# The last batch's attention across heads, set at other steps of the four queues

## What is computed

```python
def _L0_cond2_ref(x, s, ...):
    kx = modulated_linear(x, s, k_aff_w, k_aff_b, k_w, k_b)
    kx = kx.reshape(B, N, H, D)          # 16 heads of 16 features
    q = k = v = kx
    scores = jnp.einsum('bnhd,bnjd->bnhj', q, k) / math.sqrt(D)
    A = jax.nn.softmax(scores, axis=-1)
    out = jnp.einsum('bnhj,bnjd->bnhd', A, v).reshape(B, N, F)
    return modulated_linear(out, s, o_aff_w, o_aff_b, o_w, o_b)
...
for i in range(DEPTH):                   # DEPTH = 6
    x = attn_layer(shift_tokens(x), ...) + x
    x = ffn_layer(shift_tokens(x), ...) + x
```

## Time and profile before

| what | value |
| --- | --- |
| median of 3 runs | 3278.33 us |
| lowest and highest run | 3275.71 and 3279.32 us |
| span of the profiled execution | 3280.4 us |
| TensorE busy | 3087.2 us (94%) |
| VectorE busy | 2638.4 us (80%) |
| ScalarE busy | 2534.1 us (77%) |
| GpSimd busy | 2084.0 us (64%) |

### The profile page before, as it was taken

The page is one execution under the profiler, slowest core; times in us unless marked ns, Lnnn a source line. Parts: engine busy times, 40 slices in busy tenths (PEclk is TensorE's granted clock), DMA queues, the critical chain, the costliest instruction groups (busy, mean ns, idle before and its releaser), DMA issues. The chain is left out here.

```text
span 3280.4 us, 80720 instructions
## 1 busy us (share of the span) xinstructions
PE 3087.2 (94%) x29936; PEld 2736.1 (83%) x29936; DVE 2638.4 (80%) x5117; ACT 2534.1 (77%) x7059; POOL 2084.0 (64%) x1536
## 2 busy tenths in 40 slices
PE   5898886689999999999999999999999999999997
PEld 4666664479998999989999989999899998999996
DVE  3378888878789888788878898878988878888884
ACT  2787885478787888788888888888788887888784
POOL 5347655776666666666666676667676767666661
PEclk8888996799999999999999999999999999999998
DMA  3111100110001000001100011000100000110000
GB/s 128 55 36 49 59 4 7 42 36 11 2 2 34 25 26 2 2 21 33 31 2 2 11 34 39 1 2 2 37 26 22 2 1 21 33 31 7 8 5 26
DMA packets 27780, 75.04 MB, mean 23 GB/s; under 512 B 4120, under 2 KB 9848, under 8 KB 27256
## 3 DMA queue, kind: packets, MB, share of 16 engines
q1 hardware_dynamic: 22224, 52.63, 5.1%
q0 software_dynamic: 4864, 16.78, 1.6%
q10 hardware_dynamic: 304, 0.47, 0.1%
HBM read 65.68 MB, written 4.19 MB: 21 GB/s over the span
## 5 line engine op out<-in xcount | busy, mean ns | idle before, releaser
L1596 POOL TENSOR_TENSOR turned<-by_cos,turned 128x512 f32<-128x512 f32 x384 | 494.5, 1288 | 827.5 <-DVE turned L2101 827.0
L1600 POOL TENSOR_TENSOR rnorm<-norm,half 128x8 f32<-128x8 f32 x384 | 789.1, 2055 | 0.0
L1883 ACT ACTIVATE prob<-ps_s,ebias,rnorm 128x128 f32<-128x128 f32 x1536 | 681.8, 457 | 64.9 <-DVE ebias L2122 64.2
L2115 DVE TENSOR_REDUCE negmax<-ps_s 128x8 f32<-128x1024 f32 x192 | 235.0, 1224 | 284.0 <-PE ps_s L1698 283.9
L1892 ACT ACTIVATE prob_t<-ps_t 128x512 f32<-128x512 f32 x384 | 230.3, 600 | 223.4 <-PE ps_t L1707 218.8
L2130 DVE TENSOR_TENSOR prob<-prob,rinv 128x512 f32<-128x512 f32 x384 | 375.8, 979 | 13.1
L1642 PE MATMUL ps_qk<-w_hi,x_hi 128*128 128x512 f32 x768 | 336.8, 438 | 18.8 <-DVE turned L2101 12.2
L1787 PE MATMUL ps_f<-hid_hi,w_hi 128*128 128x256 f32 (+1 forms) x1056 | 309.3, 293 | 5.7 <-DVE hid_lo L2176 5.6
L1883 ACT ACTIVATION_READ_ACCUMULATOR prob<-ps_s,ebias,rnorm 128x1 f32 x1536 | 311.1, 203 | 0.0
L1642 PE MATMUL ps_qk<-w_lo,x_hi 128*128 128x512 f32 x768 | 305.8, 398 | 0.0
L1642 PE MATMUL ps_qk<-w_hi,x_lo 128*128 128x512 f32 x768 | 305.7, 398 | 0.0
(11 more groups left out here) (289 smaller groups left out, 9779.6 us busy)
## 6 DMA issues: line engine op xcount, KB each, us to landing
w_raw<-in_w_qkv SPq DMA_DIRECT2D x24, 768.0 KB, 4.8
w_raw<-in_w SPq DMA_DIRECT2D x12, 693.0 KB, 4.0
w_raw<-in_w_o SPq DMA_DIRECT2D x12, 512.0 KB, 3.4
w_raw<-in_w SPq DMA_DIRECT2D x6, 768.0 KB, 4.4
x_tok<-in_x SPq DMA_DIRECT2D x8, 256.0 KB, 2.7
kept<-x_t SPq DMA_DIRECT2D x8, 256.0 KB, 2.0
w_raw<-kept SPq DMA_DIRECT2D x8, 256.0 KB, 3.1
out<-rows_out SPq DMA_DIRECT2D x8, 256.0 KB, 2.2
```

The source lines that it names most:

```text
L1596: G.tensor_tensor(turned[:, k, :], by_cos[:, :], turned[:, k, :], ALU.add).then_inc(s["turned"], 1)
L1600: G.tensor_tensor(rnorm[:, i % RR, :], norm2[:, k, :], half[:, :], ALU.pow).then_inc(s["rnorm"], 1)
L1883: last = A.activation(prob[:, k, h, :], half_bank(h % 2, k)[:, T(h // 2)], ACT.Exp, bias=ebias[:, i // NU % 2, k, h:h + 1], scale=rnorm[:, ...
L2115: V.tensor_reduce(negmax[:, k, :, :].rearrange("p u (c o) -> p o u c", o=2), ps_s[:, :, :].rearrange("p o (u c k) -> p o u c k", u=NU, c=2 ...
```

## The change

Nothing is added and nothing taken away. Lines of the form `for c in lates(...)` get other offsets and other places in the lists of POOL, TensorE, ScalarE and VectorE. The offsets, before and after (VectorE unless another engine is named):

| piece | unit 0: before, after | unit 1: before, after |
| --- | --- | --- |
| `head_prod` 0, 1, 2, 3 | 0 0 0 1, 0 0 0 1 | 2 2 3 4, 3 3 4 5 |
| `head_scores` 0, 1, 2, 3 | 0 0 1 1, 0 0 1 1 | 3 4 4 4, 3 4 5 5 |
| `head_mirror` (ScalarE) | 2, 0 | 5, 6 |
| `head_peak` | 2, 1 | 7, 6 |
| `head_exp` (ScalarE) | 2, 1 | 8, 6 |
| `head_weights` | 2, 3 | 8, 8 |
| `head_out` 0, 1, 2, 3 (POOL) | 4 6 6 8, 4 5 6 7 | 10 10 13 15, 10 11 13 15 |
| `head_out` 0, 1, 2, 3 | 3 4 7 8, 4 5 7 9 | 9 9 13 13, 9 12 14 14 |

The other offsets stay (`turn_k` 1, `flip_heads` 13 and `heads_out` 14 of TensorE, `flip_heads` 13 and `heads_out` 15 of ScalarE), but the places in a step change. An offset alone doesn't place a piece: one at the head of a step's list stands just behind one at the foot of the step before. The core of the diff, of which the rest is like it:

```diff
@@ pe @@
         for t in range(STEPS):
+            for c in lates(t, 14):
+                heads_out(c)
             for q in passes(t, 20):
...
-            for c in lates(t, 14):
-                heads_out(c)
             for i in units(t, 0):
                 project(i)
@@ dve @@
-            for c in lates(t, 9):
-                head_out(c, 1, 1)
+            for c in lates(t, 12):
+                head_out(c, 1, 1)
```

More of the change, by code:

```diff
@@ L1606, in pool @@
         for t in range(STEPS):
[L1607 to L1608 removed]
+            for c in lates(t, 1):
+                turn_k(c)
+            for c in lates(t, 10):
+                head_out(c, 1, 0)
+            for c in lates(t, 15):
+                head_out(c, 1, 3)
+            for c in lates(t, 5):
+                head_out(c, 0, 1)
+            for i in units(t, 3):
+                rotated(i)
+            for c in lates(t, 7):
+                head_out(c, 0, 3)
+            for c in lates(t, 11):
+                head_out(c, 1, 1)
+            for q in passes(t, 25):
+                hidden_lo(q, 0)
+            for c in lates(t, 4):
+                head_out(c, 0, 0)
+            for q in passes(t, 20):
+                inverse_root(q)
+            for c in lates(t, 13):
+                head_out(c, 1, 2)
             for c in lates(t, 6):
                 head_out(c, 0, 2)
[L1611 to L1630 removed]
             for q in passes(t, 27):
@@ L1833, in pe @@
                 mean_mm(q)
+            for c in lates(t, 13):
+                flip_heads(c)
             for q in passes(t, 14):
@@ L1837, in pe @@
                 w_o_mm(q, 1)
-            for c in lates(t, 13):
-                flip_heads(c)
             for q in passes(t, 21):
@@ L1967, in act @@
                 soften(i)
-            for c in lates(t, 2):
-                head_mirror(c, 0)
             for q in passes(t, 20):
@@ L1979, in act @@
                 attend(r)
-            for c in lates(t, 2):
-                head_exp(c, 0)
             for q in passes(t, 21):
@@ L1999, in act @@
                 flip_prob(i)
+            for c in lates(t, 0):
+                head_mirror(c, 0)
             for layer in layers(t, 16):
                 w1_high(layer, 0)
+            for c in lates(t, 13):
+                flip_heads(c)
             for layer in layers(t, 18):
@@ L2005, in act @@
                 w_o_high(layer, 1)
-            for c in lates(t, 15):
-                heads_out(c)
             for q in passes(t, 17):
                 square(q)
-            for c in lates(t, 13):
-                flip_heads(c)
+            for c in lates(t, 6):
+                head_exp(c, 1)
             for layer in layers(t, 20):
@@ L2015, in act @@
                 gelu(q, 1)
+            for c in lates(t, 1):
+                head_exp(c, 0)
     def dve():
@@ L2317, in dve @@
                 attend_lo(r)
-            for c in lates(t, 3):
-                head_prod(c, 1, 2)
+            for c in lates(t, 0):
+                head_prod(c, 0, 2)
             for q in passes(t, 22):
@@ L2323, in dve @@
                 linear_lo(q)
-            for c in lates(t, 7):
-                head_out(c, 0, 2)
             for c in lates(t, 1):
-                head_scores(c, 0, 3)
+                head_peak(c, 0)
     sp()
```

124 lines of the change are left out of this document (52 added, 72 removed).

## The result

| what | before | after |
| --- | --- | --- |
| median of 8 runs | 3277.02 us | 3282.86 us |
| lowest and highest run | 3270.48 and 3280.89 us | 3273.36 and 3287.09 us |
| ratio, 95% interval | | 1.0025, 1.0013 to 1.0037 |
| repeated, medians of 17 and 12 runs | 3274.97 us | 3278.58 us |
| ratio of the repeat, 95% interval | | 1.0015, 1.0000 to 1.0029 |

The forecast was 3278.1 us, range 3273.9 to 3281.5, and "no difference" at 0.93. The time is outside the range, on the slow side, and the interval of the first comparison lies above 1. The change is a small loss: by the two ratios 0.15 to 0.25%, so 5 to 8 us (the medians themselves lie 5.84 and 3.61 us apart). The miss of the range by 1.4 us is itself no measure, since the repeat, at 3278.58 us, lies inside it while the kernel before came out at 3274.97; what has to be explained is the difference.

What follows compares the result with a forecast made beforehand. VectorE bounds 590 to 645 us, a two-step loop paces 645 to 710, TensorE is 98.5% busy after. Terms -0.7 + 0.5 + 0 = -0.2 us give 3278.1 us against the runs' median 3278.33; range 3273.9 to 3281.5.

Steps and rivals of the forecast that it cites:

- Part 1: Steps 8 to 10: `soften(3)` and `rotate(9)` start earlier, TensorE's wait for POOL's keys goes; 0.7 us gained, bounds 0 to 0.94.
- Part 2: Step 14: `heads_out` first in TensorE's queue, so the transposes of `flip_qk(12)` come later; +0.5 us, bounds 0 to 0.8.
- Part 3: Steps 0 to 7: VectorE's reordered late work costs about nothing; 0, bounds 3.0 us lost to 1.1 us gained.
- The collision with `turn_k`: Start of the layers: the first `head_prod` stands 1.0 us for POOL's `turn_k`, the state's cast 0.8 less; sum 0.2 us higher.
- the term 0: Steps 0 to 7: the moved VectorE work was taken to cost 0 us in sum.
- fewer collisions: Steps 0 to 7: pieces might run into fewer collisions, gaining one late sum, 1.1 us; the gain bound.
- the 2.12 us of `weigh(2)`: `weigh(2)` on VectorE, slow beside POOL's late product; product leaves, but `soften(2)` waits for scores anyway, so given nothing.
- the bound of 3.0: Steps 0 to 7: 2.09 + 0.87 = 3.0 us lost if all of it opens as idle time.
- the rival that named the clock: Steps 8, 10, 12: less TensorE waiting keeps the clock up, three projections give 4.2 us, 3273.9 us; chance 0.14.
- Slower from the start: Steps 0 and 1: first square later than `rotate(0)` can be, second `project` delayed; 3.0 us lost, 3281.1 us; chance 0.2.
- The moves cancel: Step 10's wait comes back one step later, leaving only Part 2's loss; 3278.8 us; chance 0.2.

Runs made afterwards that it cites:

- a_again: The changed kernel profiled again with no edit; 3278.58 us (median of 12 runs), `rotate(20)` +5.34 us against before.
- a_pe: The changed kernel with TensorE's queue as before (transposes of `flip_qk(12)` ahead of `heads_out`); 3278.88 us, `rotate(20)` +7.40 us.
- b_fill: The kernel before with POOL's late products of the last batch replaced by constant fills that only write; 3275.46 us, `rotate(20)` +1.20 us.
- a_pool: The changed kernel with POOL's products of unit 0 back where the kernel before has them; 3270.11 us, `rotate(20)` +0.42 us.
- a_fill: The changed kernel with POOL's late products of the last batch replaced by constant fills that only write; 3278.57 us, `rotate(20)` +3.84 us.
- best: a_pool with `head_weights` of unit 1 moved behind `soften(2)`; 3275.80 us (median of 12 runs), ratio to before 1.0009.
- a_o2: The changed kernel with only POOL's third product of unit 0 moved ahead of `rotated(3)`; 3294.68 us, `rotate(20)` +5.62 us.
- late: The kernel before with only the later half of the change, steps 0 to 5 and TensorE's queue as before; 3280.47 us, `rotate(20)` +0.37 us.
- b_again: The kernel before profiled again with no edit; 3268.89 us, `rotate(20)` +0.34 us against its first profile.
- the pair of fills: The kernels before and after, each with POOL's late products of the last batch replaced by constant fills; 3275.46 and 3278.57 us.

## Why the prediction was wrong

**What bounds the kernel.** Read right: from 710 us on nothing changed, and between 590 and 645 us VectorE bounds. That reading should have warned: where VectorE bounds, each of its instructions that takes longer is on the path.

**Part 1, forecast -0.7 us: right in its steps, too large in size.** From `rotate(7)` to `rotate(9)` it takes 13.84 us now, against 14.36: 0.52 us gained in this profile and 0.21 in a_again. VectorE, `rotate(7)`, the split with the wait for ScalarE's copy that was foreseen, and `rotate(9)`:

```profile
648.85 0.69 DVE L2095 TENSOR_TENSOR by_cos<-ps_qk,cos_t 128x512 f32<-128x512 f32 x1
...
658.74 1.22 DVE L2054 TENSOR_TENSOR wo_lo<-w_raw,wo_hi 128x1024 fp32r<-128x1024 f32 x1 [0.44 <-ACT wo_hi L1920]
...
662.69 0.68 DVE L2095 TENSOR_TENSOR by_cos<-ps_qk,cos_t 128x512 f32<-128x512 f32 x1
```

The idle time ahead of `soften(4)` is 1.22 us, forecast about 1.3, where it was 2.46:

```profile
674.49 1.22 DVE L2115 TENSOR_REDUCE negmax<-ps_s 128x8 f32<-128x1024 f32 x1 [1.22 <-PE ps_s L1698]
```

TensorE's wait of 2.42 us for POOL's keys ahead of `flip_qk(8)` is gone too: it follows at 655.66 us with 1.14 us of idle for ScalarE. Each step of this part held. What it left out is a wait that took the place of the work that went from ahead of `rotate(8)`:

```profile
653.92 0.69 DVE L2095 TENSOR_TENSOR by_cos<-ps_qk,cos_t 128x512 f32<-128x512 f32 x1 [1.20 <-ACT sq L1856]
```

**Part 2, forecast +0.5 us: right.** `heads_out` waits 1.16 us now (0.19 before) with the transposes behind it, `rotate(14)` is 0.43 us later against `rotate(13)`, and a_pe, without the move, has -0.01.

```profile
688.78 1.99 PE L672 MATMUL bank_m<-o_t,o_w 128*128 128x256 f32 x8 [1.16 <-ACT o_t L921]
690.61 0.60 PE L1667 MATMUL ps_t<-ident,turned 128*128 128x128 f32 x4
```

**Part 3, forecast 0, bounds -1.1 to +3.0: wrong, and this is the step that failed.** Its first claims held. `rotate(0)` opened 0.37 us earlier, so the moved products do fit ahead of it. The collision with `turn_k` came as the prediction had it, and at the size worked out: the two products took 2.93 us (forecast 2.09 + 1.0) while the state's cast took 0.42 instead of 1.26 us:

```profile
587.11 2.93 DVE L1259 TENSOR_TENSOR prod<-kx 128x1024 f32<-128x1024 f32 x2
589.96 0.42 DVE L2083 CAST x_hi<-state 128x514 fp32r<-128x514 f32 x1
```

What failed is the term 0 itself, "I take **0**", and the step to it: that VectorE's instructions keep their lengths at their new places, or gain by "fewer collisions". The prediction read the 2.12 us of `weigh(2)` as a price that goes away when POOL's product leaves, and gave that nothing, as `soften(2)` waits for scores anyway. By itself this is borne out: b_fill took 1.43 us off that division and had `rotate(7)` at +0.07. But it did not ask where the product arrives. POOL's products of the first unit had all moved or met other work, and none was laid against the VectorE instruction at its new place. Doing so gives what the rows after show: the first two products run on into the split of group 2 and push POOL's `turned` into it (1.86 + 0.95 us held), the third runs into `head_prod(1, 3)` (1.85 us), the first of unit 1 into `take_x(1)` (2.03 us). At `rotate(7)`, where this part ends, the kernel is 7.6 us late, and 8.9 in a_again, beyond the bound of 3.0. That bound was of the wrong kind as well: it was for idle time, and nothing in it stood for instructions that get longer.

**How the 4.9 us come about.**

- `rotate(0)` to `rotate(2)`: +1.6 us, the new order of VectorE's pieces (held: the pair `head_prod(1, 0)` and `(1, 1)`, 2.60 against 2.08 us). It is given back: in a_pool `rotate(3)` is at -0.88.
- `rotate(2)` to `rotate(4)`: +3.1 us, where `w_hi`, `w_lo` and `prod` took 4.7 us more, less 1.5 us of sums that now stand elsewhere. The loss goes when POOL's products go (a_fill +0.57, a_pool +0.28 at `rotate(4)`).
- `rotate(4)` to `rotate(5)`: +1.64 us: a small sum that now stands here, 0.4 us, and 1.24 us in which VectorE waits for scores ahead of `soften(1)`. TensorE had waited 3.27 us ahead of `project(5)`, which then ran at the low level, 4.17 us instead of 2.35. This is the rival that named the clock, with the sign turned. After and then before, its first and fourth matmul, and VectorE's wait in after:

```profile
627.61 0.76 PE L1642 MATMUL ps_qk<-w_hi,x_hi 128*128 128x512 f32 x1 [3.27 <-DVE turned L2101]
...
629.02 0.63 PE L1642 MATMUL ps_qk<-w_hi,x_hi 128*128 128x512 f32 x1
```
```profile
627.33 0.48 PE L1642 MATMUL ps_qk<-w_hi,x_hi 128*128 128x512 f32 x1
...
628.12 0.39 PE L1642 MATMUL ps_qk<-w_hi,x_hi 128*128 128x512 f32 x1
```
```profile
633.60 1.23 DVE L2115 TENSOR_REDUCE negmax<-ps_s 128x8 f32<-128x1024 f32 x1 [1.24 <-PE ps_s L1698]
```

  That the wait, and with it the hold, brought the low level on isn't shown. `project(5)` was at it, wholly or for the most part, in seven of the eight profiles with VectorE's new early order, with 3.27 us of wait ahead of it, with 1.42 (a_fill), with 0.17 (a_pool, the row below) and with none (best). It was at the high level in the eighth (a_o2, after 1.38 us) and in all six with the old order. In a_pool 0.69 us were lost here.

```profile
615.00 0.77 PE L1642 MATMUL ps_qk<-w_hi,x_hi 128*128 128x512 f32 x1 [0.17 <-DVE turned L2101]
```

- `rotate(6)` to `rotate(7)`: +1.64 us: `x_lo` +2.03, `head_weights(1)` moved here +1.2, the division of `weigh(2)` -1.43. From (7) to (8) it is 1.0 us less: `head_weights(1)` and a late sum are missing there, 2.2 us, and the wait of 1.20 us for ScalarE's square stands in their place.
- `rotate(7)` to `rotate(9)`: -0.5 us in all, part 1. `rotate(13)` to `rotate(14)`: +0.43, part 2.
- `rotate(11)` to `(12)`: -1.27 us, and (17) to (20): -1.1 us: `project(12)` and `project(18)` ran at the high level, 2.35 us, where before they took 3.86 and 3.85. In a_pe, with the same loss up to there, they didn't, and 7.40 us stayed. So this return of 2.4 us is the clock's, and the order of the queues up to there doesn't force it; with it the loss is 4.9 to 5.3 us, without it 7.4. That the total came out as near to the forecast as it did is in part this luck.

**The rivals.** "Slower from the start" named 3.0 us and idle time ahead of `rotate(0)`. The sign came true, the mechanism didn't: `rotate(0)` was earlier. "The moves cancel" named +0.5 us. That a_pool and late end at +0.42 and +0.37 us, no more than b_again has without any change (+0.34), doesn't bear it out: late has no part 2, and a_pool stood at +2.48 at `rotate(11)` and came down by the two projections at the high level. The cleaner number is best, which met the low level at both, as before did: +0.44 at `rotate(11)`, +0.88 at `rotate(20)`, with part 2's 0.43 in it.

**What stays open.** Which level of the clock a projection meets: two runs with the same queues and the same times differ, and yet `project(5)` went with VectorE's order in 13 of 14 profiles. So how much of the loss behind `rotate(4)` is the holds' and how much the clock's. Why the stage ahead ends within a range of 20 us. The rest of the 2.6 us in the pair of fills.

## What to carry to other kernels

When a POOL instruction that reads SBUF is moved, write down what VectorE does at its new place, not only what it leaves. An instruction with two SBUF inputs or a copy in SBUF is held there to the product's end, unless it was the first to start, and where VectorE bounds, that goes into the time nearly in full; a reduction was never held (those of 128x1024 took 1.20 to 1.23 us in each run). And where an earlier stage varies from run to run, count from the first instruction of the stage that the change touches: a difference of 0.5 us can be seen so in single profiles, where the clock fell the same way, while 12 and 17 totals left an interval 0.3% wide.

## What was not expected of the hardware

- The hold doesn't depend on the size of the held instruction: one of 128x8 elements went from 0.17 to 2.17 us beside a product of 2.33, and one of 128x514 from 0.69 to 2.72 beside a product of 2.46. Each lasted to the end of the product and a little beyond.
- POOL pays as well: its `turned` of 128x512 took 1.99 us instead of 1.28 in the middle of the split. And where VectorE began first, POOL alone paid. In the kernel before `w_lo` began at 616.51 us and took its 1.76 us, while this product of POOL's, otherwise 0.61 us, took 2.14:

```profile
616.59 2.14 POOL L1603 TENSOR_TENSOR turned<-turned,rnorm 128x256 f32<-128x256 f32 x1
```

- A POOL fill, which only writes, holds nothing: `w_lo` took 1.76 us beside it.
- The same queue, with the same waits and the same times up to it, met `project(12)` at 2.36 us in one run and at 3.86 us in another.
